# A decoder layer on one core: the maxima of the cross attention four per step, less expert work per step, and one part of the experts' squares on GpSimd

## What is computed

```
x = _layernorm(x + _L0_attn_ref(x, ...), axis=-1)              # causal self attention, 16 heads of 16
x = _layernorm(x + _L0_xattn_ref(x, ctx_1024, ...), axis=-1)   # attention to rows picked from a context
x = _layernorm(x + _L0_ffn_ref(x, ...), axis=-1)               # eight experts, two chosen for each token
```

```
logits = xf @ router_w.T;  probs = jax.nn.sigmoid(logits)
topw, sel = jax.lax.top_k(probs, TOP_K)          # TOP_K = 2, then normalised and spread to `combine`
h = jnp.square(jax.nn.relu(jnp.einsum('td,edw->tew', xf, W1e)))   # widths 256 x4, 512 x4
out = jnp.einsum('ted,te->td', jnp.einsum('tew,ewd->ted', h, W2e), combine)
```

## Time and profile before

| | us |
|---|---|
| runs, lowest / median / highest | 1342.40 / 1346.37 / 1346.80 |
| the profiled execution, its own time | 1341.76 |
| its span (first to last instruction) | 1340.1 |
| PE busy | 1182.8 |
| DVE busy | 906.4 |
| ACT busy | 673.7 |
| POOL busy | 175.8 |
| mean granted TensorE clock | 0.925 of full speed |

### The profile page before, as it was taken

How to read it: one execution, slowest core, us unless ns; L and a number is a source line. 1 busy time by engine, 2 the same in 40 slices (tenths; PEclk the granted TensorE clock), 3 DMA queues, 4 the chain that set the end, 5 groups by cost and what they waited for, 6 DMA issues and landing times. The chain is left out here.

```text
span 1340.1 us, 18687 instructions
## 1 busy us (share of the span) xinstructions
PE 1182.8 (88%) x6943; PEld 640.1 (48%) x6943; DVE 906.4 (68%) x1799; ACT 673.7 (50%) x951; POOL 175.8 (13%) x167
## 2 busy tenths in 40 slices
PE   6855999999999999865998698799998999999796
PEld 3522233333333333244787222356655665677685
DVE  4464998898899887045799699566665656633543
ACT  1320256666666666831443145365644664575462
POOL 2222111021021000152000462000000000000000
PEclk9785799999999999986999579899999999999899
DMA  6224077910000000030200241000000000000000
GB/s 242 83 64 88 25 81 82 111 13 2 1 1 1 1 1 2 1 132 27 71 24 1 87 152 43 25 1 13 13 23 18 13 13 13 17 1 1 16 1 18
DMA packets 45049, 51.03 MB, mean 38 GB/s; under 512 B 8122, under 2 KB 40506, under 8 KB 44954
## 3 DMA queue, kind: packets, MB, share of 16 engines
q1 hardware_dynamic: 44954, 49.78, 16.5%
HBM read 37.64 MB, written 11.53 MB: 37 GB/s over the span
## 5 line engine op out<-in xcount | busy, mean ns | idle before, releaser
L627 DVE TENSOR_REDUCE self_piece_max<-self_max 128x1 f32<-128x512 f32 (+3 forms) x640 | 349.6, 604 | 53.0 <-PE self_max L529 25.5
L594 ACT ACTIVATE self_probs<-self_scores 128x1024 f32<-128x1024 f32 (+3 forms) x320 | 274.1, 896 | 193.8 <-PE self_scores L548 192.8
L529 PE MATMUL self_max<-stack_k,stack_q 96*128 96x512 bf16 (+3 forms) x640 | 210.5, 368 | 12.3 <-DMA stack_k<-kparts 6.4
L1623 DVE TENSOR_REDUCE cross_piece_max<-banks 128x1 f32<-128x512 f32 x256 | 165.0, 685 | 76.6 <-PE banks L1441 76.0
L1591 ACT ACTIVATE cross_probs<-banks 128x1024 f32<-128x1024 f32 x128 | 128.6, 1018 | 137.7 <-PE banks L1502 136.9
L548 PE MATMUL self_scores<-stack_q,stack_k 98*128 98x512 bf16 (+3 forms) x640 | 170.5, 350 | 4.3 <-DMA stack_q<-self_shift 3.0
L559 PE MATMUL self_out<-self_probs,V 128*17 128x512 f32 (+3 forms) x1280 | 148.8, 537 | 2.6 <-ACT self_probs L594 2.0
L529 PEld LDWEIGHTS self_max<-stack_k,stack_q 96*128 96x128 bf16 x640 | 62.3, 98 | 181.1 <-DVE self_piece_max L627 130.8
L94 PE MATMUL banks<-w_first,hid_first 128*128 128x256 f32 x384 | 119.9, 312 | 11.6 <-DVE hid_rest L1703 7.2
L1441 PE MATMUL banks<-kx_few,stackx 97*128 97x512 bf16 x256 | 97.2, 425 | 18.4 <-issue 7.3
L1703 DVE TENSOR_TENSOR hid_rest<-o_tok,hid_first 128x512 fp32r<-128x512 f32 x96 | 65.8, 687 | 65.1 <-ACT o_tok L1574 65.1
(11 more groups left out here) (219 smaller groups left out, 1709.8 us busy)
## 6 DMA issues: line engine op xcount, KB each, us to landing
stack_q<-qparts SPq DMA_DIRECT2D x96, 64.0 KB, 8.7
stackx<-xparts SPq DMA_DIRECT2D x96, 64.0 KB, 2.3
o_tok<-in_w SPq DMA_DIRECT2D x8, 768.0 KB, 4.8
stack_k<-kparts SPq DMA_DIRECT2D x18, 256.0 KB, 13.8
qparts<-parts SPq DMA_DIRECT2D x8, 384.0 KB, 2.5
kparts<-parts SPq DMA_DIRECT2D x8, 384.0 KB, 2.5
xparts<-xparts_sb SPq DMA_DIRECT2D x8, 384.0 KB, 2.7
xT_sb<-in_xT SPq DMA_DIRECT2D x4, 512.0 KB, 8.1
```

Source lines behind the costliest of these rows:

```text
L529: mm = nc.tensor.matmul(slot[:, 0:pc["w"]], pc["lhsT"], pc["rhs"], start=True, stop=not pc["diag"])
L594: nc.scalar.activation(probs[:, i % 3, 2 * pair:2 * pair + 2, st["off"]:C], ps[:, 2 * pair:2 * pair + 2, st["off"]:C], ACT.Exp, scale=SCAL ...
L627: nc.vector.tensor_reduce(piece_max[:, u % 2, pc["row"], pc["at"]:pc["at"] + 1], slot[:, 0:pc["w"]], AX.X, ALU.max).then_inc(side_read, 1)
L1623: nc.vector.tensor_reduce(piece_max[:, u % 2, pc["row"], pc["at"]:pc["at"] + 1], slot[:, 0:pc["w"]], AX.X, ALU.max).then_inc(side_read, 1)
```

## The change

Three things, and all of them in the block of the cross attention and experts.

1. `just_in_time` takes the place of `schedule` for this block. The 16 pieces of unit 0, its turn, and now five pieces of unit 1 come ahead of the first step. Step 0 has seven pieces, each later one four (2, 1 and 1 in its thirds) until all 256 are given. A turn comes two thirds after the last piece of its unit, which puts it in the second third of step 4u-2.
2. `PACE` = 0.9 multiplies the pace, so that a third of a step gets a tenth less credit for expert work and norms.
3. `rest` is done by GpSimd, in one stream with the powers of the norms, in the order of the list. VectorE has no `rest` any more.

```
+PACE = 0.9
...
+            def just_in_time(steps, works):
+                per, length = len(works[0]["pieces"]), len(steps) // len(works)
+                maxima = [("piece", u, k) for u in range(len(works)) for k in range(per)]
+                given = per + per // 3
+                before = maxima[0:per] + [("turn", 0)] + maxima[per:given]
...
+                    want = min(len(maxima), per + -(-per * (i + 3) // length))
+                    new = maxima[given:want]
+                    given = max(given, want)
+                    for k in range(3):
...
+                        mine = new[(k * len(new) + 2) // 3:((k + 1) * len(new) + 2) // 3]
+                        thirds[i][k] += mine
+                        late += [(2, ("turn", item[1])) for item in mine if item[2] == per - 1]
...
-                pace = per_chunk * NC / (len(steps) * 3)
+                pace = PACE * per_chunk * NC / (len(steps) * 3)
...
-            plans = [merge(*schedule(*plan(kx_few, lambda t: vx_few[:, t, :], FEW))),
+            plans = [merge(*just_in_time(*plan(kx_few, lambda t: vx_few[:, t, :], FEW))),
...
+                        for item in [it for step in slots for slot in step for it in slot]:
+                            if item[0] in ("stats", "fstats"):
...
+                            elif item[0] == "rest":
+                                h = tile_at[item[1:]]
+                                pool.wait_ge(square_ready, h + 1)
+                                nc.gpsimd.tensor_tensor(hid[1][:, h % HR], relu[:, h % 2], hid[0][:, h % HR].bitcast(F32),
+                                                        ALU.subtract).then_inc(hid_ready, 1)
...
-                            elif kind == "rest":
-                                h = tile_at[item[1:]]
-                                dve.wait_ge(square_ready, h + 1)
-                                nc.vector.tensor_tensor(hid[1][:, h % HR], relu[:, h % 2], hid[0][:, h % HR].bitcast(F32),
-                                                        ALU.subtract).then_inc(hid_ready, 1)
```

25 lines of the change are left out of this document (17 added, 8 removed).

## The result

The changed kernel takes 1322.37 us (median of 4 executions, 1320.82 to 1328.39), the kernel before 1344.68 us beside it (4 executions, 1342.4 to 1346.8). The ratio is 0.9843 with a 95% interval of 0.9806 to 0.988, so it is 22 us faster. The prediction said 1312 us, range 1299 to 1328: the time is in the range, though one of the four executions is not, and the gain is two thirds of the forecast. The profiled execution of after took 1323.07 us.

The account below looks back on a forecast made before the run. TensorE was taken as the bound from step 20 on; before, VectorE's maxima, waits and slow clock added time. Savings of 18.3 + 9.5 + 5.5 = 33.3 us gave 1308.5 or 1313.1, stated as 1312 us, range 1299 to 1328.

Parts of the forecast that it names:

- the late shift: Rival: in four units before step 18 TensorE waits up to 2 us for the shift, costing 8 us: 1320; chance 0.15.
- Start: Block's beginning to step 18: 21.5 us sooner, less 3.2 us for moved pieces, net 18.3 us; bounds 10 and 23.
- Lower pace: Steps to tail: 16.7 us of TensorE work moves, costed at nothing because both are TensorE-bound.
- the rival of 1330: Rival: a chain of scores and exponential holds the steps, so the moved 16.7 us come on top in the tail; chance 0.09.
- The two waits of 2.7 us: Tail: `y` waits of 2.75 and 2.68 us behind VectorE's norm work and gates go, within 8.9 us gone.
- Middle: Steps 20 to 63: 6.5 us of waits and 3 us of slow clock gone, together 9.5 us; bounds 0 and 20.
- I take half, 6.5 us: Steps 20 to 63: half of TensorE's 13.7 us of waits for VectorE go once VectorE has no `rest`.
- Tail: After the steps: 8.9 us of waits and slow clock gone, 3.4 us lost to later `rest`, net 5.5; bounds 0 and 9.
- The five places: Tail: four `y` behind four `hid` and the last `y`, each 0.68 us later through GpSimd, 3.4 us.
- GpSimd as the bound (0.04): Rival: VectorE's `y` and GpSimd's `rest` hold each other up, `rest` lengthens to 3.4 us: 1371; chance 0.04.

Follow-up runs that it names:

- part 1 alone: Kernel before with only the maxima just in time, pace 1.0 and second part of the squares on VectorE: 1327.23 us, ratio 0.9881.
- part 2 alone: Kernel before with only the pace of 0.9, order of maxima and engine of the second parts unchanged: 1328.34 us, ratio 0.9898.
- parts 1 and 2: Changed kernel with the second part of the squares given back to VectorE: 1314.21 us, ratio 0.9792.
- the half-column kernel: Changed kernel, but from the seventh tile on GpSimd subtracts only 256 of 512 columns, the others not computed: 1316.31 us, ratio 0.9794.
- parts 1 and 3: Changed kernel with pace 1.0, second part of the squares still on GpSimd: 1339.29 us, ratio 0.9970.

## Why the prediction came out as it did

The sum can be put in the order of the parts, since each term belonged to one of them.

| part | forecast | measured alone | measured on the others |
|---|---|---|---|
| 1, maxima just in time | 18.3 | 16.0 | |
| 2, pace 0.9 | 8.9 (tail) | 13.7 | 12.0 (on 1) |
| 3, GpSimd | +6.1 (9.5 steps, -3.4 tail) | -7.3 | -6.9 (on 1, 2) |
| sum | 33.3 | | 21.1 |

Measured numbers are differences of ratios times 1344.5 us, each good to some 4 us. The 3 us of clock in the steps are put with part 3, since the prediction had them lie behind the waits for VectorE. Of the miss of 12 us, part 3 makes 13 and part 1 makes 2, and part 2 gave 3 more than was forecast. That the time is in the range is in part luck: it lies nearer to the 1320 of the late shift, which didn't come, than to the 1312 of the forecast.

**Start: right.** The forecast had step 18 21.5 us sooner (its own numbers, 849.7 - 0.8 - 827, make 21.9). From the block's beginning, before it was 849.7 - 754.5 = 95.2 us, now it is 829.63 - 755.89 = 73.7. The five pieces took 3.02 us of wait to 0.54. A unit takes 12.4 us, in the range of 11.5 to 12.5. The granted clock rose at 774 us and not at 785. Step 4 was forecast for 783.3 and its exponential began at 784.55 us, in a block that began 1.4 us later. The stack loads are not waited for. That it fits to the tenth is luck: the same stage took 73.7 to 76.5 us in the eleven kernels that have part 1. The late shift (0.15) didn't come: the one wait for `cross_shift` is the 0.54 us. That net 16.0 and not 18.3 arrived with part 1 alone lies within the error.

**Lower pace: costed at nothing and rightly so, gain larger than forecast.** The 16.7 us did move at no cost (steps 20 to 63 lost 23.6 us in part 2 alone), which settles the rival of 1330. The two waits of 2.7 us and their slow stretches went. Not foreseen was that the steps would gain by it beyond the work moved: in part 2 alone their waits fall from 20.6 to 15.8 us and the time at half clock from 17 to 7. Nor was it foreseen where the transposed tokens of the last chunk would now stand: I took their wait for unchanged at 1.65 us, and it is 3.27, behind two tiles on ScalarE (part 1 alone has it too, at 3.18). My order listing showed VectorE at this place and not ScalarE, which had the queue.

**Middle: the step that failed.** "I take half, 6.5 us": the waits that the profile puts down to VectorE would fall with VectorE's load. Steps 20 to 63 were to take 357.4 - 16.7 - 9.5 + 3.2 = 334.4 us and took 341.7. Counted in the trace, 25 matmuls of `hid` and 79 of `y` left this stage and 19 pieces came, 11.3 us of work less where the forecast had 13.5. The other 5 us of the miss are its term of 9.5: waits fell by 3.3 us and not 6.5, and the time at half clock from 17 to 14 us, which is 1.7 us and not 3. Of the 13.7 us of waits in question 8.6 are left (17.3, less 4.1 for `x_sb` L1701 and 4.6 for `x2T_rest`), so 5.1 us did go, near the forecast. But parts 1 and 2, in which VectorE still has its `rest`, have 9.1 us of them left: the new order and the lower pace did it, and of my reason, the lighter VectorE, 0.5 us remains. And the waits that I took for unchanged, the norm and the transposed tokens, rose from 6.9 to 8.7 us. The waits for the norm alone are 2.9 us before, 3.2 in parts 1 and 2 and 4.1 in the change, and there VectorE was held up by GpSimd. The prediction looked for such a hold-up in the other direction and at `y` alone. It had quoted a rule on who interferes with whom, exceptions included, and then asked it of `y` only, not of the norm and the gates. For the steps part 3 should have stood in the sum with nothing, as relief and hold-ups came out even. The waits were forecast at 10 to 15 us and were 17.3.

**Tail: the second term that was mis-sized.** The five places were the right ones, and GpSimd was later by about 0.6 us at each: 0.91 - 0.28 and 3.68 - 3.07, 3.1 us together where 3.4 was forecast. What was left out is what stands behind a wait. In the earlier trace rows I had charged waits of 2.7 us with a slow stretch each; for the 0.68 us added to a wait I charged none. Here the tail has 15 us at half clock, and 5 in parts 1 and 2, up to 5 us of time. The tail was to take 122.0 + 16.7 - 5.5 = 133.2 us in the windows used here (126 from step 64 on), and took 139.4; with VectorE's own subtraction it is 132.0. Its waits grew from 11.5 to 12.5 us, where the forecast had them fall by 2.1, and its time at half clock from 12 to 15 us, where two stretches of 3.5 were to go. Beyond the work that moved, the tail lost some 2 us, where the bounds of its term were a gain of 0 to 9. That this clock is the consequence of the longer waits is what the numbers suggest and no run shows by itself: the half-column kernel has short waits and 14 us at half clock in its profiled tail.

**GpSimd as the bound (0.04):** refuted. Its mean is 1286 ns, none of its subtractions takes over 1310, and VectorE's maxima (685 ns) and updates of `x_sb` are not slower than before, 482 against 481 ns:

```profile
L1738 DVE SCALAR_TENSOR_TENSOR x_sb<-banks,mix,x_sb 128x256 f32<-128x256 f32 x128 | 61.5, 482 | 128.9 <-PE banks L95 127.8
```

The 32 updates that start during a subtraction take 484 ns. So with these operands the two engines don't hold each other up, which agrees with the Trainium skill, SBUF — State Buffer, section "Who interferes with whom". With the operands of the norm and of some instructions of the gates, none of them in PSUM, GpSimd did hold VectorE up, as shown above. The rival had the right pair of engines and the wrong one of the two. The rule of the Trainium skill's GPSIMD Engine Reference, section "Engine selection", that elementwise work belongs on VectorE, is borne out by this case (1286 against 687 ns) and more strongly than I weighed it. By that rule the prediction had 1314 us, 2 above the forecast; following it for part 3 was worth some 7 us. GpSimd wasn't short of time (it was idle 272 us waiting for the squares); but its result is waited for, and VectorE waits beside it.

## What to carry to other kernels

Ask of work moved to an idle engine how long its result takes to appear, who waits for it, and whom it stops meanwhile, not how busy the engines are. Here the move took 66 us off VectorE, made each result 0.6 us later, stretched a few instructions of VectorE from 0.4 to 1.4 us, and cost 7 us. After such a move compare the longest and not only the mean time of the other engine's instructions: its means for maxima and updates showed nothing. A wait put down to an engine is only won by a lighter load if other work was queued in front of the step that is waited for; look at that engine's rows just before it and, for a chain of several engines, at each one's. And when work stands before a last phase that has too little to cover its waits, leaving a little more of it for then (a pace of 0.95 instead of 1) can be worth 1%. The best version here is parts 1 and 2 without part 3, 1314.2 us, ratio 0.9792, with 0.95 and 0.9 alike.

## What was not expected of the hardware

- GpSimd held up VectorE: its fp32 subtraction of two SBUF tiles stretched VectorE's 128x256 norm instruction from 0.41 to as much as 1.48 us, and, in parts 1 and 3, a `CAST` of 128x8 from 0.17 to 1.15 us. Its maxima and updates, which read PSUM, ran beside it at their usual time: those that began during a subtraction took 691 and 484 ns, the others 684 and 482.
- GpSimd's subtraction took 1286 ns for 512 columns and 736 for 256, in the change and in its half-column form. Half of the columns costs 57% of the time. If it is a line, 186 ns of it don't depend on the columns (an estimate from these two).
- The same wait of 3.27 us, at the same `x2t`, was followed by 6.9 us at half clock in the change (from 1224.5 us on), by 3.4 in the kernel with VectorE's subtractions in the tail, and by none in parts 1 and 2. The windows right behind the wait, of the change and of parts 1 and 2 (columns as the earlier trace rows):

```profile
1224.50:1231.40 6.90, 6.13 (x15) 3.61 (x16) 0.62 (x2) 2.32 (x4) 1.45 (x2) 0.51 0.00 0
```

```profile
1221.70:1228.60 6.90, 6.88 (x40) 5.21 (x41) 1.64 (x4) 4.05 (x8) 0.00 (x0) 1.00 0.00 0
```

- Executions of one kernel differ in the same way: parts 1 and 2 had a mean clock of 0.942 or 0.943 in four executions (1312.2 to 1314.6 us) and 0.937 in two (1317.4 and 1318.8 us). Differences of 4 us between orders should not be explained from one profile.
